# Moving a layer norm's last two VectorE steps to TensorE and ScalarE in a fused convolution and Mamba kernel

## The reference

```
y1, y2 = b1_w y + b1_b, b2_w y + b2_b      # y: convolved image, products over channels
g  = gelu(y1) * y2
gn = (g - mean_c(g)) / sqrt(var_c(g) + 1e-6) * ln_w + ln_b    # mean and variance over the 128 channels
x1 = x + gn
```

## Time and profile before

| what | value |
|---|---|
| median of 3 runs | 14103.46 us (14099.97 to 14105.63) |
| the profiled execution | 14102.87 us, its span 14101.0 us |
| mean granted TensorE clock | 0.872 of full speed |
| VectorE busy | 13476.1 us (96%) |
| GpSimd busy | 13248.2 us (94%) |
| ScalarE busy | 12099.3 us (86%) |
| TensorE busy | 11209.7 us (79%) |
| DMA queue q1 | 58.7% of 16 engines' span |

### The profile page before, as it was taken

One profiled execution on the slowest core, in us unless ns is written; L12 is line 12 of the kernel. 1 busy time (PEld: TensorE's weight loads), 2 busy tenths in 40 slices (PEclk: granted clock), 3 DMA queues, 4 the chain that ended last, 5 costly groups with the idle time before them and its releaser, 6 DMA issues.

```text
span 14101.0 us, 163967 instructions
## 1 busy us (share of the span) xinstructions
PE 11209.7 (79%) x33024; PEld 3328.2 (24%) x33024; DVE 13476.1 (96%) x12083; ACT 12099.3 (86%) x24489; POOL 13248.2 (94%) x3076
## 2 busy tenths in 40 slices
PE   7788777787787878778787878777787878788787
PEld 2222222222222222222222222222222222222221
DVE  7999999999999999999999999999999999999999
ACT  7888888888888888888888888888888888888888
POOL 6999999999999999999999999999999999999999
PEclk8888888888888888888888888888888888888887
DMA  5656565556656565655566565655556565656555
GB/s 131 144 137 143 140 150 137 144 138 145 144 142 145 136 147 141 145 139 142 141 146 145 138 147 136 149 138 143 143 139 145 143 144 137 145 138 148 140 140 118
DMA packets 1068261, 1992.06 MB, mean 141 GB/s; under 512 B 123649, under 2 KB 124730, under 8 KB 1067066
## 3 DMA queue, kind: packets, MB, share of 16 engines
q1 hardware_dynamic: 1065786, 1979.41, 58.7%
q10 hardware_dynamic: 1280, 0.02, 0.0%
HBM read 1626.62 MB, written 352.32 MB: 140 GB/s over the span
## 4 chain that ended last, share of the span: by engine, by line
POOL 56%; issue 35%; DVE 4%; ACT 3%; PE 2%; POOLq 0%; ACTq 0%; DVEq 0%; DMA 0%; SPq 0%
POOL hq L973 40%; POOL dbx L965 16%; DVE hq L861 2%; ACT ps_a L592 1%; DVE dbx L844 1%; PE ps_acc L417 0%; PE ps_b L405 0%; PE pp L384 0%; ACT dbx L606 0%; ACT L552 0%; PE pp L325 0%; PE pp L361 0%; DVE pp L820 0%; POOLq L963 0%; PE pp L376 0%
## 5 line engine op out<-in xcount | busy, mean ns | idle before, releaser
L973 POOL TENSOR_TENSOR hq<-hq,c_rep 128x2048 f32<-128x2048 f32 x2048 | 9258.7, 4537 | 740.9 <-ACT carry L611 733.2
L861 DVE TENSOR_TENSOR_SCAN hq<-ps_a,dbx 128x512 f32<-128x512 f32 x8192 | 9442.4, 1204 | 122.4 <-ACT dbx L606 79.8
L592 ACT ACTIVATE ps_a<-dt_rep,A_neg 128x512 f32<-128x512 f32 x8192 | 5627.3, 687 | 1463.7 <-DVE hq L861 1408.5
L965 POOL TENSOR_TENSOR dbx<-dtx_rep,b_rep 128x2048 f32<-128x2048 f32 (+1 forms) x1024 | 4080.8, 3985 | 90.9 <-DMA dtx_rep<-dtx_d 90.9
L844 DVE TENSOR_TENSOR dbx<-dtx_rep,ps_b 128x2048 f32<-128x2048 f32 (+1 forms) x1280 | 2626.6, 2052 | 244.9 <-PE ps_b L405 244.9
L606 ACT ACTIVATE dbx<-ps_a,dbx,carry 128x1 f32<-128x1 f32 x7168 | 2504.0, 349 | 238.6 <-POOL dbx L965 137.1
L417 PE MATMUL ps_acc<-hq,dsum 128*32 128x512 f32 x16384 | 2356.5, 649 | 167.7 <-POOL hq L973 165.6
L325 PE MATMUL pp<-xin,diag 128*128 128x504 f32 (+3 forms) x4608 | 2214.0, 608 | 6.0 <-ACT diag L637 6.0
L405 PE MATMUL ps_b<-dbl,bsel 41*128 41x512 f32 x2560 | 1476.2, 657 | 373.6 <-DVE dbx L844 201.8
L361 PE MATMUL pp<-x,W_taps 128*128 128x512 f32 x768 | 660.6, 957 | 988.3 <-DVE x L815 639.2
L325 PEld LDWEIGHTS pp<-xin,diag 128*128 128x128 f32 x4608 | 793.2, 189 | 1398.4 <-issue 1398.4
(11 more groups left out here) (117 smaller groups left out, 9996.7 us busy)
## 6 DMA issues: line engine op xcount, KB each, us to landing
dtx_rep<-dtx_d SPq DMA_DIRECT2D x2048, 256.0 KB, 5.5
dt_rep<-dt_d SPq DMA_DIRECT2D x2048, 256.0 KB, 5.6
c_rep<-bc_d SPq DMA_DIRECT2D x1024, 256.0 KB, 5.5
b_rep<-bc_d SPq DMA_DIRECT2D x1024, 128.0 KB, 2.9
dtx_d<-sp SPq DMA_DIRECT2D x256, 512.0 KB, 2.8
dt_d<-dt SPq DMA_DIRECT2D x256, 512.0 KB, 6.0
out<-o SPq DMA_DIRECT2D x128, 512.0 KB, 3.5
xin<-in_x SPq DMA_DIRECT2D x192, 320.0 KB, 8.5
```

The lines of the kernel that those rows point to most:

```text
L592: A(ps_a[:, BANK[i], :], dt_rep[:, q // NQ, g, :], ACT.Exp, scale=A_neg[:, q // NQ, q % NQ, g:g + 1]).then_inc(exp_done, 1)
L861: v.tensor_tensor_scan(hq[:, q % HQ, g, :], ps_a[:, BANK[i], :], dbx[:, slot(q), g, :], 0.0, ALU.mult, ALU.add).then_inc(scan_done, 1)
L965: g.tensor_tensor(dbx[:, slot(q), m:, :], dtx_rep[:, d, m:, :], b_rep[:, c % 2, q % NQ // 2, :].unsqueeze(1).to_broadcast([P, DG - m, T]), ...
L973: g.tensor_tensor(quad, quad, c_rep[:, c % 2, q % NQ, :].unsqueeze(1).to_broadcast([P, DG, T]), ALU.mult).then_inc(cmul_done, 1)
```

## The change

VectorE multiplies g by 1/sqrt(var) and nothing else; TensorE does the centring a second time with the weights folded in (`cw` = center x diag(ln_w), made once at the start), and adds x by a product with the identity into the same bank; ScalarE reads the bank out with ln_b as bias. The 1/sqrt goes to pp[2], not sq. `scale_gate` stands at step 30 of the chunk before the one in which `norm` stood. VectorE's half of quad 3 stands behind scan 8 and behind the y_gate, not behind scan 7. The core of the diff:

```diff
+PE_X1, ACT_X1 = 0, 2
-DVE_NORM, DVE_Y1, DVE_DT, DVE_Y0, DVE_GATE = 0, 8, 16, 24, 23
+DVE_NORM, DVE_Y1, DVE_DT, DVE_Y0, DVE_GATE = 30, 8, 16, 24, 23
-PE_SHARED, DVE_SHARED = 6, 7
+PE_SHARED, DVE_SHARED = 6, 8
...
@@ TensorE @@
+            def step_x1(b, c):
+                pe.wait_ge(scaled, b * CH + c + 1)
+                mm(pp[:, 2, :], cw[:], gbuf[:], start=True, stop=False)
+                mm(pp[:, 2, :], w["ident"][:], xin[:, c % 2, W:W + T], start=False, stop=True).then_inc(x1_mm, 1)
...
@@ TensorE's chunk(b, c, end), behind select_b for quads s + 2 and 3 @@
+                    if u == PE_X1 and c + 1 < end:
+                        step_x1(b, c + 1)
...
@@ ScalarE @@
-                A(sq[:], sq[:], ACT.Exp, scale=-0.5).then_inc(rstd_done, 1)
+                A(pp[:, 2, :], sq[:], ACT.Exp, scale=-0.5).then_inc(rstd_done, 1)
+            def evac_x1(b, c):
+                act.wait_ge(x1_mm, b * CH + c + 1)
+                if c % CH == 2 and not (isinstance(b, int) and b * CH + c < CH):
+                    act.wait_ge(fin_done, CH * b)
+                A(x1_cols(c), pp[:, 2, :], ACT.Identity, bias=w["vec0"][:, 3:4]).then_inc(x1_done, 1)
...
@@ ScalarE's chunk(b, c, end), behind decay u + RA @@
+                    if u == ACT_X1 and c + 1 < end:
+                        evac_x1(b, c + 1)
...
@@ VectorE @@
-            def norm(b, c):
-                dve.wait_ge(rstd_done, b * CH + c + 1)
-                v.scalar_tensor_tensor(pp[:, 2, :], pp[:, 2, :], w["vec0"][:, 2:3], sq[:], ALU.mult, ALU.mult).then_inc(t2_done, 1)
-            def add_input(b, c):
-                dve.wait_ge(t2_done, b * CH + c + 1)
-                v.scalar_tensor_tensor(x1_cols(c), pp[:, 2, :], w["vec0"][:, 3:4],
-                                       xin[:, c % 2, W:W + T], ALU.add, ALU.add).then_inc(x1_done, 1)
+            def scale_gate(b, c):
+                dve.wait_ge(rstd_done, b * CH + c + 1)
+                v.tensor_tensor(gbuf[:], pp[:, 2, :], gbuf[:], ALU.mult).then_inc(scaled, 1)
...
@@ VectorE's chunk(b, c, end), behind scan(b, c, u) @@
-                    if u == DVE_SHARED:
-                        weigh_inputs(b, c, SHARED)
                     if c and u == DVE_Y1:
                         y_gate(b, c - 1, 1)
+                    if u == DVE_SHARED:
+                        weigh_inputs(b, c, SHARED)
...
-                        if u == DVE_NORM:
-                            norm(b, c + 1)
-                            add_input(b, c + 1)
...
@@ the same, under c + 2 < end, behind gate @@
+                        if u == DVE_NORM:
+                            scale_gate(b, c + 2)
```

More of the change, by code:

```diff
@@ L113, in build_program @@
         D_diag = sb("D_diag", [P, DI, P])
+        cw = sb("cw", [P, P])
         dsum = sb("dsum", [P, DW])
@@ L183, in build_program @@
         first_done = sem("first_done")
+        cw_step, scaled, x1_mm = sem("cw_step"), sem("scaled"), sem("x1_mm")
         dt_repd = [sem("dt_repd_0"), sem("dt_repd_1")]
@@ L467, in chunk @@
                             att_heads(b + 1)
+            pe.wait_ge(cw_step, 1)
+            mm(pp[:, 2, 0:P], w["center"][:], cw[:], start=True, stop=True).then_inc(cw_step, 1)
             att_hidden(0)
             att_heads(0)
+            pe.wait_ge(cw_step, 3)
             step_conv(0, 0, 0, TAPS)
@@ L474, in _ @@
             step_var(0, 0)
+            step_x1(0, 0)
             step_xh(0, 0, 0)
@@ L714, in _ @@
             act.wait_ge(batch_done, 1)
+            act.wait_ge(cw_step, 2)
+            A(cw[:], pp[:, 2, 0:P], ACT.Copy).then_inc(cw_step, 1)
             act.preload_act_table_set(LN_EXP)
@@ L723, in _ @@
             rstd(0, 0)
+            evac_x1(0, 0)
             silu_xh(0, 0, 0)
@@ L778, in _ @@
                 v.tensor_tensor(W_taps[:, k, :], w["W_in"][:, 0:2 * P], w["cw_rows"][:, k, :], ALU.mult)
+            v.tensor_scalar(cw[:], w["ident"][:], w["vec0"][:, 2:3], None, ALU.mult).then_inc(cw_step, 1)
             v.memset(x1[:, 0:1], 0.0).then_inc(batch_done, 1)
@@ L930, in _ @@
             gate(0, 0)
-            norm(0, 0)
-            add_input(0, 0)
+            scale_gate(0, 0)
             softplus(0, 0)
@@ L935, in _ @@
             gate(0, 1)
+            scale_gate(0, 1)
             weigh_inputs(0, 0, 0)
```

## The result

The changed kernel takes 14976.65 us (median of 4 runs, 14968.25 to 14979.4), against 14104.54 us before: a ratio of 1.0618, 95% interval 1.0604 to 1.0632. It is 6.2% slower; the forecast was 14900.

The account below looks back on a forecast made before the run. VectorE (96% busy) and GpSimd (94%) bound the kernel, with a path from x1 already binding too; 7 x 3.27 + 1.9 = 24.8 us an image, x 32 = 793; 14103 + 793 + 4 = 14900, range 14480 to 15100.

Parts of the forecast that it names:

- When x1 is ready: ScalarE's read-out of x1 behind decay 5: x1 ready at 7039.87 instead of 7035.75, 4.1 us later.
- rival 2: GpSimd is ahead and x1 comes with scan 2, at 7038.5: 14590 us; chance 0.18.
- VectorE's saving: VectorE drops norm and add_input for scale_gate: 0.85 us saved a chunk, busy time down about 218 us.
- TensorE's products: The two step_x1 products, 1.1 to 2.1 us each, fit TensorE's idle time and cost nothing.
- From x1 to the y_gate: TensorE's chain from xh to the sum of quad 7, 10.95 us: scan 9 3.27 us later in an ordinary chunk.
- So a second path binds already: x1, ...: In the kernel before, x1, then 10.65 us of ScalarE and TensorE work, then VectorE's half of quad 3.
- The clock: TensorE's first products after the idle wait run at 1.2 GHz: 2.07 us an xh product, against 1.0 to 1.1.
- rival 3: TensorE's clock stays high through xh because step_x1 fills part of the idle time: 14450 us; chance 0.06.
- Rival 4: TensorE's low clock lasts through sum and z, or ScalarE's block is late for scan 9: 15150 us; chance 0.12.
- From scan 9 to the next scan 28 nothing changes.: The stretch of a chunk from scan 9 to the next scan 28 keeps its length: no change.
- The sum: Over an image, 7 x 3.27 + 1.9 = 24.8 us, x 32 = 793 us in all.
- Rival 1: Relieving VectorE, the busiest engine, makes the kernel faster: 1.81 x 256 = 463 us less, 13640; chance 0.05.

Follow-up runs that it names:

- no_input: Changed kernel without TensorE's second product of step_x1, so x is not added to x1: 14977.88 us, ratio 1.0622.
- half_first: Changed kernel with VectorE's half of quad 3 behind scan 8 but ahead of the y_gate: 14953.38 us, ratio 1.0602.
- sum_first: Changed kernel with TensorE's sum of quad 7 ahead of select_b for the half of quad 3: 14955.2 us, ratio 1.0604.
- both orders in the kernel before: Kernel before with the half of quad 3 moved behind scan 8: behind the y_gate 14142.5 us, ahead of it 14085.51 us.
- the last experiments: Half quad ahead of y_gate, two convolution taps behind dt products: kernel before 13922.1 us; changed kernel, also x1 at step 1, 14134.77 us.

## Why the prediction was right, and where it was off

- *When x1 is ready.* Right: 4.13 us later (13.42 against 9.29). GpSimd's place, measured from scan 28, did not move (11.70 against 11.69), so rival 2, in which x1 comes with scan 2, is refuted by that distance.
- *VectorE's saving.* Scan 2 ends 0.85 earlier, as worked out, and nobody can use it. The busy time fell by 99 us, not by 218. The lengths of VectorE's instructions added up fell by 186; the other 87 are overlap that is gone, since an instruction that follows a wait no longer lies over the end of the one ahead, and chunk 7 now has five waits.
- *TensorE's products.* Hidden, as said (no_input). They ran at the low level (a mean of 1052 and 1001 ns for half a product, where half a z product takes 592 in the median), which the prediction allowed for. They leave TensorE idle for 3.6 us ahead of xh, not for the "some 5" of the forecast.
- *From x1 to the y_gate.* The forecast took 10.95 from the first xh product to the end of the sum of quad 7. Over chunks 2 to 5 and 7 it is 10.79 in the mean. The chunk shown is a short one (7477.66 to 7487.90 = 10.24); the means of single chunks go from 10.55 to 11.09. The y_gate waits 2.69 against "some 3". In chunk 7 scan 9 is 3.07 later, forecast 3.27.
- *"So a second path binds already: x1, ..."* Half right. In the kernel before, TensorE's second z product waits for ScalarE's silu of the first xh, and in the changed kernel TensorE's products never do:

```profile
PE pp L384 <- ACT xh L552: 149.7, 193, 1.6
```

  The prediction read 0.15 us of this wait out of one chunk; over chunks 2 to 8 the second z product starts 0.8 later in the mean than it would right behind the first. There ScalarE's block at step 5 set the end of the path, and x1 had that much to spare. This is why 4.13 us of x1 cost an ordinary chunk only 3.5. The forecast came to nearly the same because its 10.95, the middle of two single chunks (10.47 and 11.43), is close to the 10.79 that the chain takes without the wait; two chunks could as well have misled it.
- *The clock.* The first xh product is at the low level (2.08 us) after 3.6 us of idle, in chunk 7 in all 30 images, so rival 3 fails. Rival 4's low stretch through sum and z does not show, but the low level often lasts beyond the second xh product: in chunks 3, 5 and 6 the third is at it in 22 of 30 images, in chunks 2, 4 and 7 in 8 of 30.
- *"From scan 9 to the next scan 28 nothing changes."* The step that failed. In chunk 7 that stretch grew from 29.75 to 30.10, and the gap ahead of softplus from 0.13 to 0.33 (the last row of VectorE's timeline above). The prediction had not seen this: it read the y_gate as the only end of the path from x1. Over an image the stretch behind scan 9 grew by 2.6 us, and that is the whole of what the forecast was short. For the experiments it mattered more: it is the main reason why half_first, sum_first and both orders in the kernel before missed.
- *The sum.* 24.8 us an image forecast, 27.4 measured (464.8 - 437.4). Taken at scan 9 alone, the eight delays add up to 24.8, just the forecast, in part by luck: chunk 6, where nine diagonals are made at step 0, has 4.49 and chunk 1 3.36, while chunks 2 to 5 and 7 have 2.66 to 3.47 (forecast 3.27) and chunk 8 has 1.58 (forecast 1.9). The 2.6 behind scan 9 make 83 us in 32 images; the forecast of 14900 was 77 short.
- *Rival 1* ("faster": relieve the busiest engine). The Trainium skill's page "Perfetto Trace Analysis", section "Identifying the Most-Contended Engine", names the engine of highest occupancy as the one to improve first. Here relieving VectorE by a read-out on a less busy engine cost 6.2%, and the gain of 1.3% came from a kernel whose VectorE does the same work as before: the runs go against taking that rule alone. The section that follows it, "Optimization Strategy", which has the reader look for the gaps and make their dependencies start sooner, fits what the last experiments did.

Not settled: why GpSimd's inputs of quad 1 come later in chunks 2 to 5 once the taps are moved, and why TensorE's xh products run longer at the low level in half_first and sum_first. Nor is it shown why the second part of the change costs 40 us in the kernel before; x1 to softplus takes 25.24 in chunk 7 there against 24.99, which agrees with the late half holding up the select_b behind it.

## What to carry to other kernels

A step that starts a long chain on in-order engines should be judged by when its result is ready, not by whose time it takes: here 0.85 us saved on the busiest engine was paid for with 4.1 us on the chain, because the read-out was queued behind a wait for a third engine. When an order change "must" gain and gains nothing, look for a second path that ends as late or a little later, and shorten both at once; it may show only as a small entry in the list of waits (0.33 us a chunk here), or as a gap that the list leaves out (0.13 in the kernel before). Measure distances from a fixed instruction of each chunk; they showed in one line which engine had moved and which had not.

## What the runs showed of the hardware

Taking 409 us of products out of TensorE's idle stretches lowered the mean granted clock from 0.858 to 0.842 and changed the time by 1 us of 14977: here the extra work raised the mean clock and bought nothing, since the xh products behind it took the same 46.3 us an image in both kernels. The products of step_x1 themselves ran mostly at the low level (1.90 and 1.91 us each in the chunk shown) though they follow select_b by only 0.6 us. A shorter idle stretch did help: with x1 read out at step 1, TensorE was idle for 1.2 us ahead of xh in chunk 7 instead of 3.6, and the first xh product was at the low level in 6 of 30 images instead of 30.
